# A four-layer graph network: straight-line programs, and one fp32 incidence product per graph

## The chip, the cores and the metric

The kernel runs on one core of one Trainium2 chip. The metric is device microseconds of one execution. The median of three runs before the change is 1470.65 us (1470.1 to 1474.69).

## What is computed

128 graphs of 128 nodes, 256 features each (x), and an adjacency matrix per graph (adj, 128x128). Four graph layers follow one another, each added to its input and normalised over the features:

```python
x = _layernorm(x + L0(x, adj))   # hypergraph convolution, relu, layer norm, second convolution
x = _layernorm(x + L1(x, adj))   # mean over neighbours, concatenated with x, weighted, relu
x = _layernorm(x + L2(x, adj))   # three graph convolutions
x = _layernorm(x + L3(x, adj))   # one graph convolution, relu, mask
```

The change touches the incidence part of L0. With H = (adj != 0) and w the first row of adj, the reference forms

```python
Dn = jnp.einsum('nce,ne->nc', H, w)      # node degrees
Dn = jnp.where(Dn > 0, 1.0 / Dn, 0.0)
Be = H.sum(axis=1)                       # edge sizes
Be = jnp.where(Be > 0, 1.0 / Be, 0.0)
```

and applies Dn * H * Be * H^T twice. The kernel computes the 128x128 matrix G = H * (Be * H^T) once per graph, together with the degrees as one more column, scales its rows by Dn and uses the result (GT, transposed) in both convolutions.

## The kernel before, in words

Graphs are worked in 64 pairs. The kernel is a software pipeline: in step n each stage works on pair n - LAG[stage] (lines 22 to 26), from G at lag 0 to the last norm F at lag 5. Step 0 to 2 fill the pipeline by hand (`fill` of each engine), and `body(n, k)` is one full step, with the operations of each engine written in a fixed order; nothing reorders them. Engines meet through semaphores that count pairs.

`steps` (line 185) lays the steps out: fill, then steps 3 to 7 written out, then a hardware loop over steps 8 to 59 whose body holds four steps, then steps 60 to 68 written out. Inside the loop a pair's number is a register's value; `begun`, `upto`, `first`, `active`, `bank` and `at_count` tell the two cases apart by `isinstance(pair, int)`, and SP's loads and stores address memory with it.

TensorE's order in a step is R, G, xT, H2W, Ax2, XAB, H1, AP3, P, Tr, AXB, H1W, Ax3, Gx, GP, H2, TK. All matmuls but the transposes are issued in `mm` (line 279). Two kinds occur. Rounded products (fp32r) come as hi and lo parts, three terms each (`product`). Full fp32 products take unsplit operands: Ax2, Ax3, H2, Gx, GP. G (line 307) is of the rounded kind with two terms, H (exact in fp32r) against BH hi and BH lo, 130 columns: 128 of Be * H^T, the weight w, and a column of zeros.

The operands of G(n+1) are made in step n. VectorE: `edges` writes HT (line 903), `edge_count` sums it (907), `w_high_edge_max` copies w rounded into BH (911) and takes the maximum with 1 (913), `edge_inverse` takes the inverse (921), the rest of w (923) and splits the inverse in three operations (925, 927, 928). They are interleaved with `degree_max`, `degree_recip`, `degree_inverse` and `make_Gd` of step n. GpSimd: `make_BH` (line 1233) multiplies HT by the two parts of the inverse in two operations.

What follows in a step and is named later: VectorE adds up the third norm's input behind AP3 (line 1133, n_s), computes statistics and n_shift (847); ScalarE applies the norm, giving x3 (`apply`, 586), which TensorE's Ax3 reads; then h_mean (649) on ScalarE, h_var (945) and h_veps (948) on VectorE, h_std (653) on ScalarE, h_rstd and p_f (964) on VectorE, and TensorE's GP reads p_f. GpSimd works in its order: r_lo twice, two sums of squares, A_lo, n_s (1282), h_lo, BH, x2c (1293), xb (1243), h_lo. ScalarE's `copy_A` stands before `out_XAB`, whose first copy is xbw_hi.

Of the kernel before, what the change touches and what calls it, by code (L numbers as in the profile page):

```python
# [7 lines left out]
ALU = mybir.AluOpType  # L8
# [20 lines left out]
UNROLL = 4  # L29
FIRST_IN_LOOP = 8  # L30


def build(nc, x, adjT, w1T, w2T, wab, v1, v2, v3, wk, columns, rows, eye, out):
# [3 lines left out]
    assert (C, GP_, D, DH) == (128, 2, 256, 512) and NP % UNROLL == 0 and NP > FIRST_IN_LOOP  # L37
    END = NP + LAG["F"]

    with ExitStack() as ctx:  # L40
# [30 lines left out]
        HT = sb("HT", [2, C], F32R)  # L71
        ht_count, be = sb("ht_count", [2]), sb("be", [2])
        be_r, be_parts = sb("be_r", [2], F32R), sb("be_parts", [2, 2])

        BH = sb("BH", [2, 2, C + 2], F32R)
# [34 lines left out]
        class Norm:  # L110
# [25 lines left out]
        ht_made, ht_counted, be_max, be_made, be_hi, be_lo, bh_made = (  # L136
            sem(s) for s in ("ht_made", "ht_counted", "be_max", "be_made", "be_hi", "be_lo", "bh_made"))
        dn_1, dn_2, dn_3, gd_made = sem("dn_1"), sem("dn_2"), sem("dn_3"), sem("gd_made")
        w_hi, w_lo, gt_made, gx_hi, gx_lo = (sem(s) for s in ("w_hi", "w_lo", "gt_made", "gx_hi", "gx_lo"))
# [18 lines left out]
        def begun(pair):  # L158

            return not isinstance(pair, int) or pair >= 0  # L160

        def upto(pair):

            return min(pair, NP - 1) + 1 if isinstance(pair, int) else pair + 1

        def first(n, j):

            return isinstance(n, int) and n == j

        def active(stage, n):  # L170
            return not isinstance(n, int) or 0 <= n - LAG[stage] < NP

        def bank(stage, pair):

            filling = isinstance(pair, int)
            if filling and stage == "Tr" and pair in (1, 2):
                return 3
            if filling and stage == "GP" and pair == 0:
                return 2
            if filling and stage == "xT" and pair == 0:  # L180
                return 6
            return BANK[stage]

        def steps(eng, fill, body):

            stop = NP - UNROLL
            fill()
            for n in range(FILL, FIRST_IN_LOOP):
                body(n, n)
            with eng.Fori(FIRST_IN_LOOP, stop - UNROLL + 1, UNROLL) as base:  # L190
                for k in range(UNROLL):
                    body(base + k, k)
            for n in range(stop, END):
                body(n, n)

        def at_count(p, k):

            if isinstance(p, int):
                return 16 * (p // RING + 1)
            return (p + (RING - k % RING)) * (16 // RING)  # L200
# [12 lines left out]
        def _(sp):  # L213
# [4 lines left out]
            def input_free(p):  # L218
                sp.wait_ge(pe_did["Gx"], upto(p))
                sp.wait_ge(xb_made, upto(p))  # L220
                sp.wait_ge(pe_did["G"], upto(p))
                sp.wait_ge(w_lo, upto(p))
                sp.wait_ge(a_copied, upto(p))
                sp.wait_ge(a_lo, upto(p))
# [22 lines left out]
            def body(n, k):  # L247
                if not isinstance(n, int) or n + 2 < NP:
                    input_free(n - 2)
                    if isinstance(n, int):  # L250
                        load(n + 2)
                    else:
                        sp.dma_start(at_in[:, (k + 2) % RING],
                                     adjT[bass.ds(n + 2, 1)].rearrange("a p g c -> p (a g) c")
                                     ).then_inc(at_loaded[(k + 2) % RING], 16)
                        sp.dma_start(x_in[:, (k + 2) % RING],
                                     x[bass.ds(n + 2, 1)].rearrange("a p g c -> p (a g) c")
                                     ).then_inc(x_loaded[(k + 2) % RING], 16)
                if active("F", n):
                    p = n - LAG["F"]  # L260
                    sp.wait_ge(n4.done, upto(p))
                    src = x4[(k - LAG["F"]) % 2]
                    if isinstance(p, int):
                        sp.dma_start(out[p], src[:]).then_inc(stored[(k - 5) % 2], 16)
                    else:
                        sp.dma_start(out[bass.ds(p, 1)].rearrange("a p g c -> p (a g) c"),
                                     src[:]).then_inc(stored[(k - 5) % 2], 16)

            steps(sp, fill, body)
# [5 lines left out]
        def _(pe):  # L275
# [285 lines left out]
            steps(pe, fill, body)  # L561
# [3 lines left out]
        def _(act):  # L565
# [99 lines left out]

            def split_w1(h):
                half = slice(h * 2 * C, (h + 1) * 2 * C)
                act.wait_ge(w1_loaded[h], 16)
                copy(w1T_s[0][:, :, half], w1T_f[:, :, half]).then_inc(w1_hi, 1)

            def fill():
                act.wait_ge(consts_step, 1)
                act.activation(h_std[:, 0:1], eps_c[:], ACT.Sqrt).then_inc(table_loaded, 1)
                act.wait_ge(table_loaded, 1)
                act.wait_ge(columns_loaded, 16)
# [3 lines left out]
                split_w1(1)  # L679

# [6 lines left out]
                split_gx(1, 1)  # L687
                copy_A(1, 1)
# [17 lines left out]
                split_gx(2, 2)  # L706
                act.wait_ge(v_loaded, 16 * 4)
# [8 lines left out]
            def body(n, k):  # L716
# [64 lines left out]
                if active("F", n):  # L781
                    p = n - 5
                    if not isinstance(p, int):
                        act.wait_ge(stored[(k - 5) % 2], (p - (k - 5) % 2) * 8)
                    elif p >= 2:
                        act.wait_ge(stored[p % 2], 16 * (p // 2))
                    apply(n4, p, x4[(k - 5) % 2])
# [23 lines left out]
            steps(act, fill, body)  # L811
# [3 lines left out]
        def _(dve):  # L815
# [60 lines left out]
            g_dn = psum[:, BANK["G"], 0:2 * (C + 2)].rearrange("p (g c) -> p g c", g=2)  # L876
# [28 lines left out]
            def edge_count(n, k):  # L905
                dve.wait_ge(ht_made, upto(n + 1))
                dve.tensor_reduce(ht_count[:], f(HT[:]), AX_X, ALU.add).then_inc(ht_counted, 1)

            def w_high_edge_max(n, k):
                q = n + 1  # L910
                dve.tensor_copy(BH[:, 0, :, C:C + 1], at_in[:, (k + 1) % RING, :, 0:1]).then_inc(w_hi, 1)
                dve.wait_ge(ht_counted, upto(q))
                dve.tensor_scalar(be[:], ht_count[:], 1.0, None, ALU.max).then_inc(be_max, 1)

            def edge_inverse(n, k):
                q = n + 1
                w = at_in[:, (k + 1) % RING, :, 0:1]
# [12 lines left out]
            def prep(n, k):  # L930
                edges(n, k)
                edge_count(n, k)
                w_high_edge_max(n, k)
# [77 lines left out]
            def fill():  # L1011
# [6 lines left out]
                for h in range(2):  # L1018
                    dve.tensor_scalar(xbw[1][:, :, D + h:D + h + 1], pair01, 0.0, None, ALU.mult)
                    dve.tensor_scalar(BH[:, h, :, C + 1:C + 2], pair01, 0.0, None, ALU.mult)  # L1020
# [66 lines left out]
            def body(n, k):  # L1087
# [32 lines left out]
                if active("prep", n):  # L1120
                    w_high_edge_max(n, k)
# [77 lines left out]
            steps(dve, fill, body)  # L1199
# [3 lines left out]
        def _(pool):  # L1203
# [97 lines left out]
            steps(pool, fill, body)  # L1301
# [42 lines left out]
```

## Time and profile before

| | us |
|---|---|
| median of three runs | 1470.65 |
| the profiled execution | 1472.7 |
| its span | 1470.8 |
| TensorE matmul busy | 1420.3 (97%) |
| VectorE busy | 1151.5 (78%) |
| ScalarE busy | 1051.4 (71%) |
| GpSimd busy | 889.0 (60%) |
| DMA, mean | 31 GB/s |

Busy times are shares of the whole span, with the filling (some 70 us) and the emptying (some 90 us) in them. Matmuls overlap in the record, so two starts tell more than a duration. Times in rows are us from the span's start; the number behind the time is the operation's own length.

### The profile page before, as it was taken

To read this page: it belongs to the slowest core of one execution; us is meant where nothing else is said; L and a number is where in the kernel's file an instruction comes from. 1 tells how busy PE (TensorE), PEld (TensorE's weight loads), DVE (VectorE), ACT (ScalarE), POOL (GpSimd) and SP (SyncE) were. 2 spreads that over 40 slices of the span, in tenths; PEclk is the share of its full clock that TensorE was granted. 3 is DMA by queue.
4 is the path that set the end of the run, shared out by engine and by line. 5 is a ranking of instruction groups with operands and counts; after the bars stand their busy time and mean duration, and the time that the engine had idled before them with its cause. 6 is when DMAs were issued, how large, how long until landed. Compare 5 with 4: busy or idle time off the path is not lost. (4 is left out here: it accounts for less than half of the span.)

```text
span 1470.8 us, 34536 instructions
## 1 busy us (share of the span) xinstructions
PE 1420.3 (97%) x10896; PEld 1355.6 (92%) x10896; DVE 1151.5 (78%) x4066; ACT 1051.4 (71%) x2378; POOL 889.0 (60%) x840
## 2 busy tenths in 40 slices
PE   6899999999999999999999999999999999999974
PEld 6799999999999999999999999999999999999973
DVE  6678878878878888788788788788787887887663
ACT  3577777777777777777777777777777767777853
POOL 4565675675575576566566566566566566567532
PEclk9999999999999999999999999999999999999997
DMA  4001101101101101101101101100100110110000
GB/s 135 23 12 37 37 20 37 36 18 36 36 18 36 36 18 36 36 18 36 36 18 36 36 19 34 36 25 29 36 28 25 36 30 23 36 36 9 16 15 22
DMA packets 29819, 45.45 MB, mean 31 GB/s; under 512 B 3408, under 2 KB 12240, under 8 KB 29776
## 3 DMA queue, kind: packets, MB, share of 16 engines
q1 hardware_dynamic: 29776, 44.91, 9.7%
q8 instruction: 22, 0.36, 0.1%
q14 instruction: 21, 0.17, 0.0%
HBM read 28.12 MB, written 16.78 MB: 31 GB/s over the span
## 5 line engine op out<-in xcount | busy, mean ns | idle before, releaser
L1205 POOL TENSOR_TENSOR h_lo<-h_f,h_hi 128x512 fp32r<-128x512 f32 x128 | 165.2, 1291 | 339.9 <-ACT h_hi L567 339.9
L586 ACT ACTIVATE x<-n_s,n_shift,n_rstd 128x256 f32<-128x256 f32 x384 | 208.6, 591 | 65.9 <-DVE n_shift L847 63.1
L825 DVE BATCH_NORM_STATS2 n_st<-n_s 128x6 f32<-128x256 f32 x512 | 188.1, 409 | 7.6 <-POOL n_s L1282 5.2
L581 ACT ACTIVATE n_std<-n_mv,eps_c 128x2 f32<-128x2 f32 x256 | 74.8, 292 | 158.9 <-DVE n_mv L830 158.8
L1213 POOL TENSOR_TENSOR r_lo<-r_f,r_hi 128x512 fp32r<-128x512 f32 x128 | 164.0, 1304 | 38.2 <-ACT r_hi L567 38.1
L1274 POOL TENSOR_TENSOR n_s<-tk,mask 128x512 f32<-128x512 f32 x64 | 66.7, 1042 | 168.4 <-issue 82.6
L279 PE MATMUL psum<-v_hi,h_hi 128*128 128x256 f32 x512 | 149.4, 292 | 4.9 <-issue 4.9
L591 ACT ACTIVATE h_f<-psum,columns 128x256 f32<-128x256 f32 x256 | 107.6, 472 | 54.2 <-PE psum L279 54.2
L279 PE MATMUL psum<-w2c_hi,r_hi 128*128 128x258 f32 x512 | 145.0, 283 | 0.9 <-POOL r_lo L1213 0.9
L279 PE MATMUL psum<-v_lo,h_hi 128*128 128x256 f32 x512 | 145.3, 284 | 0.0
L279 PE MATMUL psum<-w2c_hi,r_lo 128*128 128x258 f32 x512 | 144.8, 283 | 0.0
L279 PE MATMUL psum<-v_hi,h_lo 128*128 128x256 f32 x512 | 144.8, 283 | 0.0
L279 PE MATMUL psum<-w2c_lo,r_hi 128*128 128x258 f32 x512 | 144.8, 283 | 0.0
L279 PE MATMUL psum<-gx_hi,w1T_hi 128*128 128x256 f32 x512 | 143.9, 281 | 0.0
L279 PE MATMUL psum<-A_f,x 128*128 128x128 f32 x1024 | 137.7, 278 | 5.9 <-ACT x L586 4.8
L279 PE MATMUL psum<-gx_lo,w1T_hi 128*128 128x256 f32 x512 | 143.3, 280 | 0.0
L279 PE MATMUL psum<-gx_hi,w1T_lo 128*128 128x256 f32 x512 | 143.3, 280 | 0.0
L279 PEld LDWEIGHTS psum<-A_f,x 128*128 128x128 f32 x1024 | 127.3, 194 | 6.5 <-ACT x L586 5.2
L817 DVE TENSOR_TENSOR ax_lo<-psum,ax_hi 128x512 fp32r<-128x512 f32 x128 | 87.8, 686 | 27.1 <-ACT ax_hi L567 27.1
L279 PE MATMUL psum<-wab_hi,x1T_hi 128*128 128x512 f32 x256 | 107.4, 419 | 0.0
L279 PEld LDWEIGHTS psum<-v_hi,h_hi 128*128 128x128 f32 x512 | 97.8, 191 | 5.5 <-issue 5.5
L591 ACT ACTIVATE r_f<-psum,columns 128x256 f32<-128x256 f32 x256 | 99.1, 463 | 4.1 <-PE psum L279 4.1
(146 smaller groups left out, 5113.5 us busy)
## 6 DMA issues: line engine op xcount, KB each, us to landing
x_in<-x_in_dram SPq DMA_DIRECT2D x64, 256.0 KB, 2.7
out<-x SPq DMA_DIRECT2D x64, 256.0 KB, 2.0
at_in<-adjT SPq DMA_DIRECT2D x64, 128.0 KB, 2.1
x<-v_in SPq DMA_DIRECT2D x3, 256.0 KB, 5.9
n_s<-w2T_in SPq DMA_DIRECT2D x2, 256.0 KB, 3.2
r_f<-w1T_in SPq DMA_DIRECT2D x2, 256.0 KB, 4.7
h_f<-wab_in SPq DMA_DIRECT2D x2, 256.0 KB, 5.9
rows<-rows_in SPq DMA_DIRECT2D x1, 256.0 KB, 5.9
```

What stands on the lines that cost most here:

```text
L279: return pe.matmul(o, a, b, start=start, stop=stop)
L581: act.activation(nm.std[:], nm.mv[:, :, 1], ACT.Sqrt, bias=eps_c[:, 0:1]).then_inc(nm.rooted, 1)
L586: last = act.activation(dst[:, g, :], nm.s[:, g, :], ACT.Identity, scale=nm.rstd[:, g:g + 1], bias=nm.shift[:, g:g + 1])
L591: return act.activation(dst[:, m].rearrange("p g c -> p (g c)"), psum[:, BANK[stage] + extra, (m % 2) * 2 * C:(m % 2 + 1) * 2 * C], ACT.Re ...
L817: return dve.tensor_tensor(dst[1][:], src, f(dst[0][:]), ALU.subtract).then_inc(signal, 1)
L825: last = dve.bn_stats(nm.st[:, g, :], nm.s[:, g, :])
L1205: return pool.tensor_tensor(dst[1][:], src, f(dst[0][:]), ALU.subtract).then_inc(signal, 1)
L1213: pool.tensor_tensor(r_s[1][:, half], r_f[:, half], f(r_s[0][:, half]), ALU.subtract).then_inc(r_lo[h], 1)
L1274: pool.tensor_tensor(n4.s[:], tk[:], bc(mask[:], [C, 2, D], 2), ALU.mult).then_inc(tk_masked, 1)
```

## The change

`steps` writes every step out on every engine, so every pair's number is a constant. G becomes one full fp32 product per graph on an unrounded HT and an unrounded BH of 129 columns. VectorE no longer splits w and the inverse; GpSimd makes BH in one operation; the copy of w into BH moves to ScalarE (`weight_column`, behind `copy_A` in a step, and at four places of its fill). The diff, shortened:

```diff
-        HT = sb("HT", [2, C], F32R)
-        ht_count, be = sb("ht_count", [2]), sb("be", [2])
-        be_r, be_parts = sb("be_r", [2], F32R), sb("be_parts", [2, 2])
-        BH = sb("BH", [2, 2, C + 2], F32R)
+        HT = sb("HT", [2, C])
+        ht_count, be, be_inv = sb("ht_count", [2]), sb("be", [2]), sb("be_inv", [2])
+        BH = sb("BH", [2, C + 1])
...
-        def steps(eng, fill, body):
-            stop = NP - UNROLL
+        def steps(fill, body):
             fill()
-            for n in range(FILL, FIRST_IN_LOOP):
+            for n in range(FILL, END):
                 body(n, n)
-            with eng.Fori(FIRST_IN_LOOP, stop - UNROLL + 1, UNROLL) as base:
-                for k in range(UNROLL):
-                    body(base + k, k)
-            for n in range(stop, END):
-                body(n, n)
...
         # SP, input_free
-                sp.wait_ge(w_lo, upto(p))
+                sp.wait_ge(w_made, upto(p))
...
         # TensorE, G
-                pe.wait_ge(w_lo, upto(p))
+                pe.wait_ge(w_made, upto(p))
...
-                    o = psum[:, BANK["G"], g * (C + 2):(g + 1) * (C + 2)]
-                    mm(o, HT[:, g, :], BH[:, 0, g, :], True, False)
-                    last = mm(o, HT[:, g, :], BH[:, 1, g, :], False, True)
+                    last = mm(psum[:, BANK["G"], g * (C + 1):(g + 1) * (C + 1)], HT[:, g, :], BH[:, g, :],
+                              True, True)
...
+            def weight_column(n, k):
+                q = n + 1
+                act.wait_ge(at_loaded[(k + 1) % RING], at_count(q, k + 1))
+                if begun(n):
+                    act.wait_ge(pe_did["G"], upto(n))
+                copy(BH[:, :, C:C + 1], at_in[:, (k + 1) % RING, :, 0:1]).then_inc(w_made, 1)
...
         # ScalarE, body
                 if active("R", n):
                     square_r(n, k)
                     copy_A(n, k)
+                if active("prep", n):
+                    weight_column(n, k)
                 if active("XAB", n):
                     out_XAB(n, k)
...
-            def w_high_edge_max(n, k):
+            def edge_max(n, k):
                 q = n + 1
-                dve.tensor_copy(BH[:, 0, :, C:C + 1], at_in[:, (k + 1) % RING, :, 0:1]).then_inc(w_hi, 1)
                 dve.wait_ge(ht_counted, upto(q))
                 dve.tensor_scalar(be[:], ht_count[:], 1.0, None, ALU.max).then_inc(be_max, 1)
             def edge_inverse(n, k):
...
-                dve.reciprocal(be_parts[:, 1, :], be[:]).then_inc(be_made, 1)
-                dve.wait_ge(w_hi, upto(q))
-                dve.tensor_tensor(BH[:, 1, :, C:C + 1], w, f(BH[:, 0, :, C:C + 1]), ALU.subtract).then_inc(w_lo, 1)
-                dve.wait_ge(be_made, upto(q))
-                dve.tensor_copy(be_r[:], be_parts[:, 1, :]).then_inc(be_hi, 1)
-                dve.wait_ge(be_hi, upto(q))
-                dve.tensor_copy(be_parts[:, 0, :], f(be_r[:]))
-                dve.tensor_tensor(be_parts[:, 1, :], be_parts[:, 1, :], f(be_r[:]), ALU.subtract).then_inc(be_lo, 1)
+                dve.reciprocal(be_inv[:], be[:]).then_inc(be_made, 1)
...
         # GpSimd, make_BH
-                pool.wait_ge(be_lo, upto(q))
+                pool.wait_ge(be_made, upto(q))
...
-                for h in range(2):
-                    last = pool.tensor_tensor(BH[:, h, :, 0:C], f(HT[:]), bc(be_parts[:, h, :], [C, 2, C], 2),
-                                              ALU.mult)
-                last.then_inc(bh_made, 1)
+                pool.tensor_tensor(BH[:, :, 0:C], HT[:], bc(be_inv[:], [C, 2, C], 2), ALU.mult).then_inc(bh_made, 1)
```

The fill of ScalarE calls `weight_column` for pairs 0, 1, 2 and 3: ahead of its wait for the columns, behind `split_w1(1)`, behind `split_gx(1, 1)` and behind `split_gx(2, 2)`. Two VectorE operations of the fill that cleared the zero column of BH go.

## Rows read from the trace of the kernel before

**Rows 1.** Busy time by stretch: us, each engine's busy us, clock, DMA.
```profile
661.00:749.50 88.50, 88.36 (x688) 84.49 (x687) 72.12 (x255) 65.94 (x151) 55.05 (x52) 1.00 0.09 30
```

**Rows 2.** Timeline, VectorE, line 1133: start us, length us, operation.
```profile
126.94 0.69 DVE L1133 TENSOR_TENSOR n_s<-psum,x2c 128x512 f32<-128x512 f32 x1
148.76 0.69 DVE L1133 TENSOR_TENSOR n_s<-psum,x2c 128x512 f32<-128x512 f32 x1
...
1332.43 0.69 DVE L1133 TENSOR_TENSOR n_s<-psum,x2c 128x512 f32<-128x512 f32 x1
...
1376.07 0.69 DVE L1133 TENSOR_TENSOR n_s<-psum,x2c 128x512 f32<-128x512 f32 x1 [2.49 <-PE psum L279]
```

**Rows 3.** Timeline, TensorE, Gx and H2 of an ordinary step and of step 63.
```profile
725.20 1.06 PE L279 MATMUL psum<-GT,x_in 128*128 128x128 f32 x8
...
727.20 1.05 PE L279 MATMUL psum<-A_f,h1w 128*128 128x128 f32 x8
...
1382.41 1.06 PE L279 MATMUL psum<-GT,x_in 128*128 128x128 f32 x8
...
1384.17 1.05 PE L279 MATMUL psum<-A_f,h1w 128*128 128x128 f32 x8
```

**Rows 4.** Timeline, VectorE, the same ordinary step.
```profile
722.06 0.29 DVE L847 SCALAR_TENSOR_TENSOR n_shift<-n_mv,n_rstd 128x2 f32<-128x2 f32 x1
...
724.03 0.80 DVE L948 SCALAR_TENSOR_TENSOR h_veps<-h_var,eps_c 128x2 f32<-128x2 f32 x1
...
725.31 0.88 DVE L964 SCALAR_TENSOR_TENSOR p_f<-psum,h_rstd,betaW 128x256 f32<-128x256 f32 x2
```

**Rows 5.** Timeline, GpSimd, the same step.
```profile
721.14 1.20 POOL L1233 TENSOR_TENSOR BH<-HT,be_parts 128x256 fp32r<-128x256 f32 x2
...
723.54 1.27 POOL L1243 TENSOR_TENSOR xb<-x_in,b2half 128x512 f32<-128x512 f32 x1
```

**Rows 6.** DMA queues: packets, MB, share of 16 engines.
```profile
q8 instruction: 22, 0.36, 0.1%
```

**Rows 7.** Timeline, TensorE, G and xT, then Ax2 up to XAB.
```profile
710.51 0.56 PE L279 MATMUL psum<-BH,HT 128*128 128x130 f32 x4
710.91 0.65 PE L394 MATMUL psum<-ident,x 128*128 128x128 f32 x4
...
712.83 1.05 PE L279 MATMUL psum<-A_f,x 128*128 128x128 f32 x8
713.64 0.47 PE L279 MATMUL psum<-wab_hi,x1T_hi 128*128 128x512 f32 x1
```

**Rows 8.** Timeline, VectorE, from the copy of w to line 1133.
```profile
716.47 0.74 DVE L911 CAST BH<-at_in 128x2 fp32r<-128x2 f32 x1
...
718.63 0.15 DVE L928 TENSOR_TENSOR be_parts<-be_parts,be_r 128x2 f32<-128x2 f32 x1
718.86 0.69 DVE L1133 TENSOR_TENSOR n_s<-psum,x2c 128x512 f32<-128x512 f32 x1
```

**Rows 9.** Timeline, ScalarE, copy_A's second copy and the operation behind it.
```profile
715.85 0.44 ACT L567 ACTIVATE A_f<-at_in 128x256 f32<-128x256 f32 x1
716.72 0.60 ACT L567 ACTIVATE xbw_hi<-psum 128x512 fp32r<-128x512 f32 x1 [0.43 <-PE psum L279]
```

**Rows 10.** Timeline, GpSimd and VectorE, step 63, which makes no BH.
```profile
1378.30 1.30 POOL L1293 TENSOR_TENSOR x2c<-x,rows 128x512 f32<-128x512 f32 x1
...
1379.27 0.35 DVE L847 SCALAR_TENSOR_TENSOR n_shift<-n_mv,n_rstd 128x2 f32<-128x2 f32 x1
...
1381.30 0.16 DVE L948 SCALAR_TENSOR_TENSOR h_veps<-h_var,eps_c 128x2 f32<-128x2 f32 x1
```

**Rows 11.** Timeline, GpSimd and TensorE, the first 20 us.
```profile
4.62 1.19 POOL L1233 TENSOR_TENSOR BH<-HT,be_parts 128x256 fp32r<-128x256 f32 x2 [4.16 <-DVE be_parts L928]
...
16.95 2.55 POOL L1233 TENSOR_TENSOR BH<-HT,be_parts 128x256 fp32r<-128x256 f32 x2 [11.14 <-DVE be_parts L928]
...
19.55 0.66 PE L279 MATMUL psum<-BH,HT 128*128 128x130 f32 x4 [1.70 <-POOL BH L1233]
```

More of the change, by code:

```diff
@@ L28 @@
 FILL = 3
-UNROLL = 4
-FIRST_IN_LOOP = 8
 def build(nc, x, adjT, w1T, w2T, wab, v1, v2, v3, wk, columns, rows, eye, out):
@@ L36, in build @@
     KD, KH = D // C, DH // C
-    assert (C, GP_, D, DH) == (128, 2, 256, 512) and NP % UNROLL == 0 and NP > FIRST_IN_LOOP
+    assert (C, GP_, D, DH) == (128, 2, 256, 512) and NP % 2 == 0 and NP > 8
     END = NP + LAG["F"]
@@ L135, in build @@
         pe_R0 = sem("pe_R0")
-        ht_made, ht_counted, be_max, be_made, be_hi, be_lo, bh_made = (
-            sem(s) for s in ("ht_made", "ht_counted", "be_max", "be_made", "be_hi", "be_lo", "bh_made"))
+        ht_made, ht_counted, be_max, be_made, bh_made = (
+            sem(s) for s in ("ht_made", "ht_counted", "be_max", "be_made", "bh_made"))
         dn_1, dn_2, dn_3, gd_made = sem("dn_1"), sem("dn_2"), sem("dn_3"), sem("gd_made")
-        w_hi, w_lo, gt_made, gx_hi, gx_lo = (sem(s) for s in ("w_hi", "w_lo", "gt_made", "gx_hi", "gx_lo"))
+        w_made, gt_made, gx_hi, gx_lo = (sem(s) for s in ("w_made", "gt_made", "gx_hi", "gx_lo"))
         r_relu, r_hi = [sem(f"r_relu{j}") for j in range(2)], [sem(f"r_hi{j}") for j in range(2)]
@@ L158, in begun @@
         def begun(pair):
-            return not isinstance(pair, int) or pair >= 0
+            return pair >= 0
         def upto(pair):
-            return min(pair, NP - 1) + 1 if isinstance(pair, int) else pair + 1
+            return min(pair, NP - 1) + 1
         def first(n, j):
-            return isinstance(n, int) and n == j
+            return n == j
         def active(stage, n):
-            return not isinstance(n, int) or 0 <= n - LAG[stage] < NP
+            return 0 <= n - LAG[stage] < NP
         def bank(stage, pair):
-            filling = isinstance(pair, int)
-            if filling and stage == "Tr" and pair in (1, 2):
+            if stage == "Tr" and pair in (1, 2):
                 return 3
-            if filling and stage == "GP" and pair == 0:
+            if stage == "GP" and pair == 0:
                 return 2
-            if filling and stage == "xT" and pair == 0:
+            if stage == "xT" and pair == 0:
                 return 6
             return BANK[stage]
-        def steps(eng, fill, body):
-            stop = NP - UNROLL
+        def steps(fill, body):
             fill()
-            for n in range(FILL, FIRST_IN_LOOP):
-                body(n, n)
-            with eng.Fori(FIRST_IN_LOOP, stop - UNROLL + 1, UNROLL) as base:
-                for k in range(UNROLL):
-                    body(base + k, k)
-            for n in range(stop, END):
+            for n in range(FILL, END):
                 body(n, n)
         def at_count(p, k):
-            if isinstance(p, int):
-                return 16 * (p // RING + 1)
-            return (p + (RING - k % RING)) * (16 // RING)
+            return 16 * (p // RING + 1)
         def f(ap):
@@ L247, in body @@
             def body(n, k):
-                if not isinstance(n, int) or n + 2 < NP:
+                if n + 2 < NP:
                     input_free(n - 2)
[L250 to L258, printed above, removed]
+                    load(n + 2)
                 if active("F", n):
@@ L261, in body @@
                     sp.wait_ge(n4.done, upto(p))
[L262 to L269, printed above, removed]
+                    sp.dma_start(out[p], x4[p % 2][:]).then_inc(stored[p % 2], 16)
+            steps(fill, body)
             for j in range(2):
@@ L559, in body @@
                     TK(n, k)
-            steps(pe, fill, body)
+            steps(fill, body)
         @block.scalar
@@ L674, in fill @@
                 act.wait_ge(table_loaded, 1)
+                weight_column(-1, -1)
                 act.wait_ge(columns_loaded, 16)
@@ L679, in fill @@
                 split_w1(1)
+                weight_column(0, 0)
                 relu_r(1, 1, 0)
@@ L687, in fill @@
                 split_gx(1, 1)
+                weight_column(1, 1)
                 copy_A(1, 1)
@@ L706, in fill @@
                 split_gx(2, 2)
+                weight_column(2, 2)
                 act.wait_ge(v_loaded, 16 * 4)
@@ L782, in body @@
                     p = n - 5
-                    if not isinstance(p, int):
-                        act.wait_ge(stored[(k - 5) % 2], (p - (k - 5) % 2) * 8)
-                    elif p >= 2:
+                    if p >= 2:
                         act.wait_ge(stored[p % 2], 16 * (p // 2))
@@ L809, in body @@
                     root(n1, n - 1)
-            steps(act, fill, body)
+            steps(fill, body)
         @block.vector
@@ L874, in split_xbw @@
                                   f(xbw[0][:, :, 0:D]), ALU.subtract).then_inc(xbw_lo, 1)
-            g_dn = psum[:, BANK["G"], 0:2 * (C + 2)].rearrange("p (g c) -> p g c", g=2)
+            g_dn = psum[:, BANK["G"], 0:2 * (C + 1)].rearrange("p (g c) -> p g c", g=2)
             dn = g_dn[:, :, C]
@@ L906, in edge_count @@
                 dve.wait_ge(ht_made, upto(n + 1))
-                dve.tensor_reduce(ht_count[:], f(HT[:]), AX_X, ALU.add).then_inc(ht_counted, 1)
-            def w_high_edge_max(n, k):
+                dve.tensor_reduce(ht_count[:], HT[:], AX_X, ALU.add).then_inc(ht_counted, 1)
+            def edge_max(n, k):
                 q = n + 1
-                dve.tensor_copy(BH[:, 0, :, C:C + 1], at_in[:, (k + 1) % RING, :, 0:1]).then_inc(w_hi, 1)
                 dve.wait_ge(ht_counted, upto(q))
@@ L916, in edge_inverse @@
                 q = n + 1
-                w = at_in[:, (k + 1) % RING, :, 0:1]
                 dve.wait_ge(be_max, upto(q))
@@ L932, in prep @@
                 edge_count(n, k)
-                w_high_edge_max(n, k)
+                edge_max(n, k)
                 edge_inverse(n, k)
@@ L1019, in fill @@
                     dve.tensor_scalar(xbw[1][:, :, D + h:D + h + 1], pair01, 0.0, None, ALU.mult)
-                    dve.tensor_scalar(BH[:, h, :, C + 1:C + 2], pair01, 0.0, None, ALU.mult)
                 dve.tensor_copy(w2c_s[0][:, :, D:D + 1], four01)
@@ L1120, in body @@
                 if active("prep", n):
-                    w_high_edge_max(n, k)
+                    edge_max(n, k)
                 if active("G", n):
@@ L1197, in body @@
                     shift(n2, n - 2)
-            steps(dve, fill, body)
+            steps(fill, body)
         @block.gpsimd
@@ L1299, in body @@
                     lo(h2_s, h2_f[:], h2_lo)
-            steps(pool, fill, body)
+            steps(fill, body)
 def kernel(x, adj, L0_gnn_W1, L0_gnn_b1, L0_gnn_gamma, L0_gnn_beta, L0_gnn_W2, L0_gnn_b2, L1_gnn_W,
```

## The prediction

> **What bounds the kernel now.** I read the busy time by stretch first. In four steps in the middle of the run TensorE's matmuls are busy for 88.36 of 88.50 us at full clock [rows 1]: the steady part is one unbroken matmul stream, and work taken from VectorE, ScalarE or GpSimd is worth only what it takes out of that stream.
>
> Then the length of a step. The operation at line 1133 (the third norm's sum) runs once per step, always just behind the last matmul of the stage AP3, so it is a clock tick of TensorE [rows 2]. Counting steps as the code's n, the four ticks shown are steps 6, 7, 61 and 63. Steps up to 7 and from 60 on are written out. From 6 to 7 the trace has 148.76 - 126.94 = 21.82 us, from 61 to 63 it has 43.64, again **21.82 us per step**. From 7 to 61 are 54 steps, 52 of them the loop's, in 1332.43 - 148.76 = 1183.67 us, 21.92 each. Inside the loop a step is 0.10 us longer on average.
>
> Last, whether those 21.82 us hold idle time. They do, at one place. From the first matmul of Gx to the first of H2 (across GP) an ordinary step takes 727.20 - 725.20 = 2.00 us; the last step that runs these products takes 1384.17 - 1382.41 = 1.76 us [rows 3]. The missing 0.24 us is GP waiting for p_f, which VectorE makes at 725.31 and ends 0.88 us later [rows 4]. Why p_f is late shows in three rows that fit to 0.01 us. n_shift, two numbers a lane from SBUF, starts at 722.06 and ends at 722.35; GpSimd's second BH operation ends at 721.14 + 1.20 = 722.34 [rows 4, 5]. h_veps starts at 724.03 and ends at 724.83; GpSimd's xb ends at 723.54 + 1.27 = 724.81. Such small VectorE operations stand still until the GpSimd operation under way is over. n_shift gates ScalarE's x3, behind which h_mean, h_var, h_veps, h_std, h_rstd and p_f follow in a row.
>
> **The change, part by part.**
>
> *Loop written out.* 54 steps at 21.82 would be 1178.28 us; they take 1183.67 [rows 2]. Written-out steps, with the same instructions, run at 21.82 on either side of it. So **-5.4 us**. Against it stands that the instructions no longer repeat, and all 64 steps are fetched. The larger instruction queue now moves 22 packets, 0.36 MB [rows 6], for three filling steps, five written out, four in the loop and nine at the end; later it is about four times that, 1 GB/s, and the written-out steps, which have that traffic already, show no price for it. Bounds: nothing, up to the whole 5.4 given back.
>
> *G on TensorE.* Before: 2 graphs x 2 terms, 4 matmul records of 130 columns, 710.51 to 710.91, 0.40 us. After: 2 fp32 products of 129 columns. An fp32 product appears as two records: Ax2 has 4 products and shows x8, in 713.64 - 712.83 = 0.81 us [rows 7], 0.101 us a record. Four records again: 4 x 0.101 = 0.40 us, plus one column in 128. **0 us.** The Trainium skill (FP8 and Floating Point Precision, TensorE Precision Notes) counts true fp32 as four passes through the array. At one column a cycle that would be 4 x 129 columns a graph against 2 x 130 before, and 0.22 us more a step; the row gives the narrow rounded products no such advantage, so I keep to the row.
>
> *VectorE.* It loses per step the copy of w (0.74 us), the rest of w, and three operations that split the inverse, the last of which ends at 718.78 [rows 8]. All lie before the tick at 718.86, and the tick does not move: it waits for AP3, also in the last step where VectorE had stood idle for 2.49 us before it [rows 2]. **0 us**, hidden by TensorE. Everything on VectorE behind the tick keeps its place, n_shift at tick + 3.20 in particular.
>
> *ScalarE.* One more copy of 128x2 behind copy_A, whose own copy of 128x256 takes 0.44 us; the narrow one is bounded by that. ScalarE then stands idle for 0.43 us before xbw_hi, waiting for XAB on TensorE [rows 9]. **0 us**; if that cover were gone, up to 0.44 us on xbw_hi, for which AXB waits. Its waits (at_in of the next pair, G of this one) are long over: nothing queues behind it. SP's inputs wait for w_made in place of w_lo, a semaphore of two steps ago: 0.
>
> *GpSimd, and this is the delicate one.* One BH operation in place of two: -0.6 us in front of x2c and xb. Counting from the tick at 718.86: BH +2.28 to +2.89, x2c then about +2.84 to +4.13 (1.30 long in [rows 10], starting 0.05 before BH's end is recorded), xb +4.08 to +5.35. n_shift comes at +3.20. Before, a short BH was running and let it go at +3.49. Now x2c is running, and it goes at about **+4.14**: 0.65 us later. From the end of n_shift to the start of h_veps lay 724.03 - 722.35 = 1.68 us, so h_veps starts at +5.82. Now xb is over (+5.35), and h_veps takes its bare 0.16 us (as in the last step, at 1381.30 [rows 10]) where it took 0.80: it ends at +5.98. Before, it ended at 724.83, +5.97. **Two shifts of 0.65 cancel, 0.0 us per step**, p_f and GP stay. That this mechanism works with x2c is seen in the last step, which has no BH: x2c ends at 1378.30 + 1.30 = 1379.60 and n_shift, waiting since 1379.27, at 1379.62 [rows 10]. The Trainium skill (SBUF — State Buffer, on the engine side's shared port pair) has the rule for it: VectorE with two SBUF inputs and GpSimd lock the pair for the whole instruction, and the loser blocks fully. By that rule no gap opens inside x2c, and the trace agrees; a split of bandwidth would only have stretched n_shift a little. x3 is 0.65 later too, done near +5.4, about when Ax3 begins (I put that wait at 0.1 us at most; it lies ahead of GP and comes off the wait that GP has anyway). Bounds for this term: the whole stall gone, -0.24 x 60 = -14 us; or 0.1 us more a step, +6.
>
> *Filling the pipeline.* The first G waits for BH, two operations in 1.19 us at 4.62 [rows 11]: one goes (-0.6), and three VectorE splits before it, which I put at 0.15 us each by the one at 718.63 [rows 8] (-0.45), so -1.05 us. The chain behind is serial up to the second BH. That starts at 16.95, takes 2.55 (slowed by a large VectorE operation) and TensorE idles 1.70 us for it, starting G at 19.55 [rows 11]. After: -1.05, -0.5 for the splits, -1.27 for one of two: G at about 16.75, -2.8; ScalarE's GT copy behind its squares gives 0.3 back. **-2.5 us**, if the loads are in by then. Bounds -1 and -4.
>
> *Sum:* -5.4 + 0 + 0 + 0 + 0.0 - 2.5 = -7.9 us. The profiled execution took 1472.7 us (span 1470.8); the median of the runs is 1470.65, 2.05 below it. So 1464.8 against the profiled one and **1463 us** as a median.
>
> **Rivals.**
>
> *A: the stall at GP goes.* If n_shift gets in between BH and x2c, or BH ends late enough (0.3 us) to cover it, h_veps is free at xb's end, p_f comes 0.5 us earlier, and each step loses 0.24 us: 60 x 0.24 = 14.4, giving 1449. For it: the last step ran so. Against it: there x2c happened to end at +3.53; here it is to end at +4.13. 0.18.
>
> *B: the chain over x3 gets longer.* n_shift's delay is fully paid, and the gain at h_veps is smaller, or Ax3 waits visibly: 0.1 us x 60 = +6, giving 1469, no change that can be told. For it: the cancellation is of two numbers of 0.65, and any new GpSimd boundary can catch another small operation. 0.12.
>
> *C: the fp32 product is dearer than the rows of Ax2 say (slower).* The place is G, on the stream that has no slack. If an fp32 product of an odd 129 columns takes four record times and not two, 4 more of 0.101 us come in each step: 64 x 0.40 = +26, less 7.9, giving 1489. It decides from 7.9/64 = 0.12 us per step on. Against it: Ax2 at 128 columns streams at two records a product [rows 7]. The Trainium skill's four passes, named above, would give +14 and 1477. 0.07.
>
> *D: straight code doesn't save the 5.4 us.* If fetching pages costs what the branches cost, only the filling gains: 1468. The written-out steps speak against it [rows 2]. 0.05.
>
> **How the numbers follow.** Forecast 0.58, A 0.18, B 0.12, C 0.07, D 0.05. A measurement tells 0.3% (4.4 us) from no change. The forecast is 0.5% faster and its own bounds (fill -1 to -4, chain within 0.04 us a step) reach from 1459 to 1467, so 0.56 of its 0.58 counts as faster, with all of A: 0.74. Same: B, D and the rest, 0.17. Slower: C and a worse B, 0.09. The range takes in A and B, 1446 to 1469.
>
> **What will show it.** Right: ticks of line 1133 all 21.82 us apart; BH in 4 records within 0.40 us; n_shift ending with x2c, about 0.9 us long; h_veps 0.16 us; GP still behind p_f by the same wait; G of the second pair near 17 us. Wrong: steps of 21.58 (A), of 21.9 (B), of 22.0 or more with more records under BH (C), or of 21.92 (D).

## The result

Over seven runs each the median went from 1470.65 us to **1463.80 us** (1462.21 to 1466.07); the ratio is 0.9949, 95% interval 0.9938 to 0.9960, that is 5.9 to 9.1 us faster. Forecast were 1463 and a range of 1446 to 1469. The profiled execution took 1463.48 us, 9.2 below the one before, which had lain 2 us above its median.

The busy table of the kernel after (share of the span, instructions) and its DMA queues:

```profile
span 1461.7 us, 33281 instructions
...
PE 1416.2 (97%) x10896; PEld 1353.8 (93%) x10896; DVE 1080.4 (74%) x3744; ACT 1056.8 (72%) x2442; POOL 851.7 (58%) x776
...
q8 instruction: 89, 1.46, 0.4%
q14 instruction: 81, 0.66, 0.2%
```

TensorE issues the same 10896 matmul records. VectorE lost 322 instructions and 71 us of busy time, GpSimd 64 and 37 us, and hardly any of this shows in the total. Instructions are fetched by two queues of their own, q8 and q14; q8 moves four times the packets of [rows 6], 89 for 22, and q14 81 where it moved 21.

The ticks of the third norm's sum, as in [rows 2] (steps 6, 7, 11, 12, 13, 61, 63):

```profile
124.53 0.69 DVE L1108 TENSOR_TENSOR n_s<-psum,x2c 128x512 f32<-128x512 f32 x1 [1.25 <-PE psum L254]
146.36 0.69 DVE L1108 TENSOR_TENSOR n_s<-psum,x2c 128x512 f32<-128x512 f32 x1 [1.25 <-PE psum L254]
...
233.69 0.69 DVE L1108 TENSOR_TENSOR n_s<-psum,x2c 128x512 f32<-128x512 f32 x1 [1.25 <-PE psum L254]
255.62 0.69 DVE L1108 TENSOR_TENSOR n_s<-psum,x2c 128x512 f32<-128x512 f32 x1 [1.26 <-PE psum L254]
277.46 0.69 DVE L1108 TENSOR_TENSOR n_s<-psum,x2c 128x512 f32<-128x512 f32 x1 [1.25 <-PE psum L254]
...
1325.98 0.69 DVE L1108 TENSOR_TENSOR n_s<-psum,x2c 128x512 f32<-128x512 f32 x1 [1.25 <-PE psum L254]
...
1369.66 0.69 DVE L1108 TENSOR_TENSOR n_s<-psum,x2c 128x512 f32<-128x512 f32 x1 [2.47 <-PE psum L254]
```

VectorE now stands idle 1.25 us ahead of each tick: that is where its relief went. Tick 7 is at 146.36 where it was at 148.76, so the fill gave **2.4 us**. From tick 7 to 61 it is 1179.62 us where it was 1183.67: **4.05 us**, 21.84 us a step. Behind tick 63 there were 1470.8 - 1376.07 = 94.7 us, now 1461.7 - 1369.66 = 92.0: **2.7 us** that no step of the prediction had. The three sum to the span's 9.1. That the fill and the end also hold chance is told under e8 and e12.

One ordinary step of the kernel after, VectorE, GpSimd, ScalarE and TensorE in turn (the tick is at 736.03):

```profile
739.23 0.97 DVE L832 SCALAR_TENSOR_TENSOR n_shift<-n_mv,n_rstd 128x2 f32<-128x2 f32 x1
741.88 0.16 DVE L924 SCALAR_TENSOR_TENSOR h_veps<-h_var,eps_c 128x2 f32<-128x2 f32 x1
742.51 0.88 DVE L940 SCALAR_TENSOR_TENSOR p_f<-psum,h_rstd,betaW 128x256 f32<-128x256 f32 x2
...
738.31 0.63 POOL L1207 TENSOR_TENSOR BH<-HT,be_inv 128x256 f32<-128x256 f32 x1
738.88 1.30 POOL L1265 TENSOR_TENSOR x2c<-x,rows 128x512 f32<-128x512 f32 x1
740.12 1.30 POOL L1215 TENSOR_TENSOR xb<-x_in,b2half 128x512 f32<-128x512 f32 x1
...
733.34 0.23 ACT L541 ACTIVATE BH<-at_in 128x2 f32<-128x2 f32 x1
733.90 0.60 ACT L541 ACTIVATE xbw_hi<-psum 128x512 fp32r<-128x512 f32 x1 [0.33 <-PE psum L254]
...
727.70 0.61 PE L254 MATMUL psum<-BH,HT 128*128 128x129 f32 x4
728.14 0.60 PE L368 MATMUL psum<-ident,x 128*128 128x128 f32 x4
```

n_shift waits out x2c (738.88 + 1.30 = 740.18; n_shift ends at 740.20, tick + 4.17), h_veps finds GpSimd done and takes 0.16 us, and ends at tick + 6.01. Before, these were + 3.49, 0.80 us and + 5.97. The exchange is as forecast. The new copy takes 0.23 us and ScalarE still idles 0.33 behind it. G is four records, starting 0.44 us ahead of xT where it was 0.40. x3 is late by as much as n_shift, and Ax3 does wait for it: in the median of the ordinary steps Gx, the next product, starts at tick + 6.43 where it was + 6.34. GP still waits for p_f, so these 0.09 us come off its wait.

### The profile page after: what moved, and what is told of

Read it like the earlier page. It is cut to its first block and busy times, and to the rows that moved or that the text cites. A ratio compares the mean times of both kernels' runs of the same rounds, so it can differ in the third digit from the quotient of the medians.

```text
span 1461.7 us, 33281 instructions
## 1 busy us (share of the span) xinstructions
PE 1416.2 (97%) x10896; PEld 1353.8 (93%) x10896; DVE 1080.4 (74%) x3744; ACT 1056.8 (72%) x2442; POOL 851.7 (58%) x776
## 5 line engine op out<-in xcount | busy, mean ns | idle before, releaser
L254 PE MATMUL psum<-A_f,x 128*128 128x128 f32 x1024 | 142.1, 282 | 5.4 <-ACT x L560 4.8
L1108 DVE TENSOR_TENSOR n_s<-psum,x2c 128x512 f32<-128x512 f32 x64 | 44.3, 692 | 87.0 <-PE psum L254 87.0
```

The source lines that it names most:

```text
L254: return pe.matmul(o, a, b, start=start, stop=stop)
L1108: dve.tensor_tensor(n3.s[:].rearrange("p g d -> p (g d)"), flat(BANK["AP3"]), x2c[(k - 4) % 2][:].rearrange("p g d -> p (g d)"), ALU.add). ...
```

## The experiments

Each is compared with runs of the kernel before on the same chip, whose median there was between 1469.7 and 1472.9; step times come from the ticks.

**e1, the loop alone.** The kernel before with this edit and the old G:

```diff
-            for n in range(FILL, FIRST_IN_LOOP):
+            for n in range(FILL, END):
                 body(n, n)
-            with eng.Fori(FIRST_IN_LOOP, stop - UNROLL + 1, UNROLL) as base: ...
-            for n in range(stop, END): ...
```

> The kernel before with every step written out and nothing else changed. My theory (the loop costs 5.4 us spread over its steps, by three waits in the first step behind each branch): the ticks of line 1133 lie 21.82 us apart throughout, steps 7 to 61 take 1178.3 us in place of 1183.7, the median is 5.4 us below before, 1465.3. Rival (page fetching eats it, or the 22.1 us steps have another cause than the branch): 1470 to 1471, with long steps left.

Measured: 1468.18 us, ratio 0.9980 (0.9969 to 0.9990). Its ticks 7 and 61:

```profile
149.19 0.69 DVE L1127 TENSOR_TENSOR n_s<-psum,x2c 128x512 f32<-128x512 f32 x1
...
1327.71 0.69 DVE L1127 TENSOR_TENSOR n_s<-psum,x2c 128x512 f32<-128x512 f32 x1
```

1178.52 us for the 54 steps, as forecast (1178.3), and the long steps at every fourth place are gone. The whole run gained less, 1.5 to 4.6 us by the interval; the profile has 5.2 in the steps and 1.1 behind tick 63, less 0.4 in the fill. Part of the rest is TensorE's clock: the mean granted clock of the eleven runs is 0.9891, of the fifteen of before 0.9901, which is up to 1.5 us of a run (an estimate), and the trace's clock record has two stretches of 6.8 us at half clock in the fill of this run's profile, where before has two of 3.4. The remainder stays open.

**e2, G alone, with the loop.** The kernel after with the loop of before over steps 8 to 59, and the loop's register forms of the loads, stores and waits:

```diff
-            for n in range(FILL, END):
-                body(n, n)
+            for n in range(FILL, FIRST_IN_LOOP):
+                body(n, n)
+            with eng.Fori(FIRST_IN_LOOP, stop - UNROLL + 1, UNROLL) as base: ...
+            for n in range(stop, END): ...
```

> The kernel after with the hardware loop over steps 8 to 59 put back. My theory (the parts add, and the G part is worth its 2.4 us in the fill, with ordinary steps 0.02 us longer): the 7th tick is at about 146.4 as after, steps 7 to 61 take some 1185 us, the median is 1.5 to 2.5 us below before, 1468 to 1469. Rival (the G part alone also shortens or lengthens each step): 1455 or 1475.

Measured: **1507.55 us**, ratio 1.0253 (1.0233 to 1.0273). Both theories missed it by far. Two steps in four are the 21.83 of after, but the first behind each branch back takes 24.5 to 26.2, twelve in all. VectorE and TensorE around one such place:

```profile
427.35 0.13 DVE L858 SCALAR_TENSOR_TENSOR n_shift<-n_mv,n_rstd 128x2 f32<-128x2 f32 x1
430.63 0.17 DVE L854 RECIPROCAL n_rstd<-n_std 128x2 f32<-128x2 f32 x1 [3.15 <-issue]
...
432.87 0.42 DVE L1097 TENSOR_SCALAR_CACHE_REDUCE nz<-x 128x256 f32<-128x256 f32 x1 [1.23 <-issue]
...
431.70 0.66 PE L392 MATMUL psum<-ident,x 128*128 128x128 f32 x4 [2.62 <-DVE x L868]
```

And its second queue of instruction packets (packets, MB, share):

```profile
q14 instruction: 80, 0.66, 0.1%
```

The first operation of VectorE's body comes 3.15 us late, released by nothing that the profile shows, and xT on TensorE waits 2.62 us for x1. Part of the loss is the clock. Behind this idle time TensorE is granted half its clock for 3.4 us (busy table by stretch; the clock is the third number from the end):

```profile
429.00:432.50 3.50, 0.88 (x8) 0.80 (x8) 0.90 (x3) 1.65 (x6) 0.00 (x0) 1.00 0.01 2
432.50:435.90 3.40, 3.40 (x18) 3.40 (x18) 1.99 (x7) 2.09 (x4) 1.84 (x2) 0.50 0.01 2
```

Eight of the twelve long steps hold such a stretch and take 26.0 to 26.2 us; the four without take 24.5 to 24.7.

The second instruction queue moves 80 packets where the kernel before moved 21 for the same number of written-out steps: the loop fetches instructions anew on every round. Yet VectorE's body is *shorter* than before, 303 recorded instructions for 323. So a new theory: instructions are fetched in packets of fixed size (pages; here 0.66 MB in 80 packets, 8 KB each), and not the body's length but its place against their boundaries decides whether every round fetches it anew.

**e5 and e6, only the place moved.** e5 is e2 with 47, e6 the kernel before with 77 one-column memsets of VectorE in the fill, ahead of the loop. The edit of e5 against e2 (e6 has 40 and 37 at the same two places):

```diff
+                for j in range(24):
+                    dve.memset(pads[:, j:j + 1], 0.0)
                 dve.wait_ge(w2_sums, 1)
...
+                for j in range(24, 47):
+                    dve.memset(pads[:, j:j + 1], 0.0)
                 dve.wait_ge(betaW_sums, 1)
```

> The kernel of the run with the loop put back (1507.6), plus 47 tiny VectorE memsets in the fill, ahead of the loop. They move the loop's place in VectorE's program back to about where the kernel before had it; its body stays 303 recorded instructions. My theory (each branch of VectorE waits some 3 us for instruction pages because of where the body lies against page boundaries, not because of its length or of what it computes): the instruction packets of the second queue fall from 80 to about 21, the steps of 24.5 to 26.2 us become 22.1 to 22.3, and the time is 1468 to 1472 (the memsets add up to 3 us). Rival (something in the new G makes the first step behind a branch long): still about 1507.

> The kernel before plus 77 tiny VectorE memsets in the fill, which move its loop by 0.6 of a page of 128 instructions. My theory (place against the pages): its VectorE body of 323 now also straddles one page too many, the second queue's packets rise from 21 to about 80, each branch costs some 3 to 4 us more, 13 x 3 = 39, 1505 to 1515. Rival (only the changed G brings the long steps): 1471 to 1475, the price of the memsets alone.

Measured: e5 **1470.64 us** (ratio 0.9983, 0.9973 to 0.9994), e6 **1511.86 us** (ratio 1.0273, 1.0250 to 1.0296). The second instruction queue of e5:

```profile
q14 instruction: 21, 0.17, 0.0%
```

The same of e6:

```profile
q14 instruction: 82, 0.67, 0.2%
```

Instructions that do nothing, placed ahead of the loop, take 37 us away in one kernel and add 39 to the other; from tick 7 to 61 it is 1184.50 us for e2's 1223.89, and 1223.33 for before's 1183.67. So it is the place of the body, neither its length nor the new G: the loop of the kernel before was cheap by where it lay. That boundaries of pages are what the place is measured against is not shown, since only one amount of padding was tried in each kernel.

e5 is also what e2 was meant to be, G with a loop that stays cheap: its median is 2.3 us below before's on the same chip, as e2's first theory had it.

**e3, the fp32 product's price.** The kernel after with G's products issued twice:

```diff
-                for g in range(2):
+                for g in (0, 1, 0, 1):
                     last = mm(psum[:, BANK["G"], ...], HT[:, g, :], BH[:, g, :], True, True)
```

> The kernel after with both fp32 products of G issued a second time (the same result). If an fp32 product of 129 columns costs two records of 0.101 us, and TensorE's stream has no slack before AP3: +0.40 us per step, 64 x 0.40 = 26 us, 1490. If each costs four record times: +0.80 us per step, 1515. If G lies beside other work: no change.

Measured: 1481.73 us, ratio 1.0074 (1.0057 to 1.0091), which is 18 us above after for the 26 expected. G and the start of xT:

```profile
734.24 1.05 PE L254 MATMUL psum<-BH,HT 128*128 128x129 f32 x8
735.13 0.60 PE L368 MATMUL psum<-ident,x 128*128 128x128 f32 x4
```

G takes 0.89 us for 0.44. Ticks lie 22.11 us apart, only 0.27 more. GP's weights load at tick + 7.24 and not + 7.41, since BH, x2c and xb start some 0.16 us earlier against a tick that moved back (tick + 2.13 for + 2.29): 0.27 + 0.17 = 0.44 us for two products more, four record times of 0.11. Two records a product, 0.22 us, and not four; the wait at GP swallowed the rest.

That leaves why the old product of 130 columns was no cheaper, 0.40 us for four records [rows 7]. The kernel before also has fp32 products of a single column, here four records and the start of what follows:

```profile
721.54 0.50 PE L279 MATMUL psum<-ones,sq 128*128 128x1 f32 x4
721.91 0.42 PE L329 MATMUL psum<-ident,Gd 128*128 128x128 f32 x2
```

They take 0.37 us, and a rounded record of 256 columns takes 0.12. So a record costs some 0.1 us in this kernel however narrow it is; what sets that isn't shown.

**e4, the wait at GP taken away.** The kernel after with one GpSimd operation moved:

```diff
-                if active("prep", n):
-                    make_BH(n, k)
                 if active("x2", n): ...
                 if active("GP", n):
                     make_xb(n, k)
+                if active("prep", n):
+                    make_BH(n, k)
```

> The kernel after with GpSimd's BH moved behind x2c and xb in every step. My theory (GP waits for p_f because n_shift, and in the kernel before also h_veps, stand still behind a GpSimd operation): x2c ends at tick + 3.5, n_shift with it, h_veps finds GpSimd idle or in BH for at most 0.3 us, p_f at about + 5.9, GP's wait is gone, a step takes 21.58 to 21.62 us, and the median is 0.24 x 57 = 14 us below after, 1450. Rival (the wait at GP has another cause, or the next G now waits for BH): 1464 or more.

Measured: **1447.67 us**, ratio to before 0.9843 (0.9826 to 0.9860), 16 us below after. One step from its tick on, VectorE, GpSimd and TensorE:

```profile
728.25 0.69 DVE L1108 TENSOR_TENSOR n_s<-psum,x2c 128x512 f32<-128x512 f32 x1 [1.47 <-PE psum L254]
731.45 0.22 DVE L832 SCALAR_TENSOR_TENSOR n_shift<-n_mv,n_rstd 128x2 f32<-128x2 f32 x1
733.35 0.16 DVE L924 SCALAR_TENSOR_TENSOR h_veps<-h_var,eps_c 128x2 f32<-128x2 f32 x1
733.99 0.88 DVE L940 SCALAR_TENSOR_TENSOR p_f<-psum,h_rstd,betaW 128x256 f32<-128x256 f32 x2
...
730.39 1.27 POOL L1263 TENSOR_TENSOR x2c<-x,rows 128x512 f32<-128x512 f32 x1
731.62 1.29 POOL L1215 TENSOR_TENSOR xb<-x_in,b2half 128x512 f32<-128x512 f32 x1
732.87 0.61 POOL L1207 TENSOR_TENSOR BH<-HT,be_inv 128x256 f32<-128x256 f32 x1
...
734.60 1.06 PE L254 MATMUL psum<-GT,x_in 128*128 128x128 f32 x8
735.49 1.03 PE L254 MATMUL psum<-p_f,GT 128*128 128x256 f32 x4
736.36 1.05 PE L254 MATMUL psum<-A_f,h1w 128*128 128x128 f32 x8
```

p_f starts at tick + 5.74 for + 6.48, Gx to H2 takes 1.76 us, the figure of step 63 in [rows 3], and every step takes 21.56 us. This is the fastest of all kernels here.

**e10, the same in the kernel before**, with its two operations and its loop:

> The kernel before, loop and rounded G kept, with GpSimd's two BH operations moved behind x2c and xb. My theory: n_shift ends with x2c at tick + 3.5, h_veps at + 5.1 waits at most for the first BH operation (+ 5.25), GP's wait is gone in ordinary steps, 21.56 to 21.6 us each, only the steps behind a branch stay longer (about 21.9): 14 us below before, 1456 to 1459 where before shows 1470 to 1473. Rival (the wait comes back because h_veps waits for both operations, + 5.85, as late as after): 1470.

Measured: 1453.70 us, ratio 0.9873 (0.9851 to 0.9894). Its ticks 7, 11, 12 and 61:

```profile
148.59 0.69 DVE L1133 TENSOR_TENSOR n_s<-psum,x2c 128x512 f32<-128x512 f32 x1 [0.30 <-PE psum L279]
...
234.85 0.69 DVE L1133 TENSOR_TENSOR n_s<-psum,x2c 128x512 f32<-128x512 f32 x1 [0.30 <-PE psum L279]
256.41 0.69 DVE L1133 TENSOR_TENSOR n_s<-psum,x2c 128x512 f32<-128x512 f32 x1
...
1313.18 0.69 DVE L1133 TENSOR_TENSOR n_s<-psum,x2c 128x512 f32<-128x512 f32 x1 [0.30 <-PE psum L279]
```

54 steps in 1164.59 us; e4, without a loop, has 1164.24. The step with the branch is 256.41 - 234.85 = 21.56 us long, like the others: the 5.4 us that the loop cost go when GP's wait goes. They were there only because a delay of a few tenths at each branch met a chain without slack. I had expected 21.9 there. The 6 us by which the whole run is above e4's do not lie in the steps: 2.5 are in the fill (tick 7 at 148.59 for 146.13) and 2.8 behind tick 63, which is clock (e8 and e12).

**e7, GpSimd's half microsecond put back.** The kernel after with a second product of BH's shape, into a spare tile, ahead of BH:

```diff
+                pool.tensor_tensor(BH_spare[:], HT[:], bc(be_inv[:], [C, 2, C], 2), ALU.mult)
                 pool.tensor_tensor(BH[:, :, 0:C], HT[:], bc(be_inv[:], [C, 2, C], 2), ALU.mult).then_inc(bh_made, 1)
```

> The kernel after with a second GpSimd product of BH's shape, into a spare tile, ahead of BH. My theory (with one BH the wait of n_shift grows by as much as h_veps's shrinks): x2c and xb are 0.57 us later, n_shift ends at tick + 3.49 and takes 0.29 us again, h_veps waits for xb (0.80), p_f at + 6.44, steps of 21.81 to 21.82 in place of 21.84, and the time is 1 us below to 1 us above after's 1463.8. Rival (GpSimd's half microsecond matters by itself): 1475 or more if it were on the path at its length, 57 x 0.57 = 32 us.

Measured: 1465.34 us, ratio 0.9949 (0.9933 to 0.9964), and 1178.41 us from tick 7 to 61, 1.2 below after. Making BH twice on GpSimd is not slower in the steps. n_shift takes 0.30 us and h_veps 0.80 again (tick at 736.43):

```profile
739.63 0.30 DVE L833 SCALAR_TENSOR_TENSOR n_shift<-n_mv,n_rstd 128x2 f32<-128x2 f32 x1
...
741.62 0.80 DVE L925 SCALAR_TENSOR_TENSOR h_veps<-h_var,eps_c 128x2 f32<-128x2 f32 x1
```

The 21.82 us of this step, with the fp32 G in it, also say that the 0.44 us for 0.40 at G isn't paid.

**e9 and e11, VectorE's five operations put back.** The kernel after with three copies and two subtractions into spare tiles; e9 has all five ahead of the inverse, e11 at the places where the kernel before had its own (one ahead of the maximum, four behind the inverse):

```diff
+                dve.tensor_copy(spare[2][:], w)
+                dve.tensor_tensor(spare[3][:], w, w, ALU.subtract)
+                dve.tensor_tensor(spare[4][:], w, w, ALU.subtract)
...
                 dve.reciprocal(be_inv[:], be[:]).then_inc(be_made, 1)
```

> The kernel after with five small VectorE operations put back ahead of the inverse (three copies and two subtractions of w's shape into spare tiles). My theory (VectorE's relief is worth nothing in a step, since line 1133 waits for AP3, and some of the fill's gain is these operations): steps of 21.84 as after, tick 7 about 0.5 to 1 us later than after's 146.4, 1464 to 1465. Rival (the relief counts): 5 x 0.15 to 0.7 us a step on the path, at least 57 x 0.8 = 45 us, 1509.

> The kernel after with five small VectorE operations put back at the places where the kernel before had its own: a copy ahead of the maximum, the rest behind the inverse, so that GpSimd's BH is not held. My theory (the relief is worth nothing as long as the last of them ends before AP3 does, and here it must, as it did in the kernel before, some 0.1 us ahead): steps of 21.84, tick 7 at 146.4, 1463 to 1466. Rival (they cost whenever they are there, as in the run with five ahead of the inverse): steps of 23.07, 1535. Between: the last one misses the end of a GpSimd operation and waits for n_s (1.29 us), steps of about 23.

Measured: e9 **1535.76 us** (ratio 1.0427, 1.0407 to 1.0447), steps of 23.07; e11 1462.84 us (ratio 0.9940, 0.9920 to 0.9961), 1179.33 us from tick 7 to 61, as after. e9, VectorE and GpSimd up to the tick:

```profile
564.13 0.15 DVE L909 TENSOR_TENSOR spare<-at_in 128x2 f32<-128x2 f32 x1
564.20 1.25 DVE L910 TENSOR_TENSOR spare<-at_in 128x2 f32<-128x2 f32 x1
565.38 0.15 DVE L911 RECIPROCAL be_inv<-be 128x2 f32<-128x2 f32 x1
565.45 0.66 DVE L1115 TENSOR_TENSOR n_s<-psum,x2c 128x512 f32<-128x512 f32 x1
...
564.14 1.29 POOL L1261 TENSOR_TENSOR n_s<-n_s,x 128x512 f32<-128x512 f32 x1
```

The last of the five has two columns. It slips behind the start of GpSimd's n_s and waits out all of it (564.14 + 1.29 = 565.43; it ends at 565.45), and the tick, till then a clock of TensorE, is now VectorE's. Each step costs 1.23 us more for one missed boundary. In their old places the same five are free, though the last of them ends only 0.08 us ahead of the tick.

**e8 and e12, before and after once more**, for the stretch behind tick 63:

> The kernel before once more, for a second profile. The steps should repeat to 0.02 us (steps 7 to 61 in 1183.7 us). If the 2 us by which its profiled execution lies above the median are TensorE's clock while the pipeline empties, this profile shows either the same half-clock stretches and 94.8 us behind tick 63, or none between and 92 us.

> The kernel after once more, for a second profile. Steps of 21.84 (steps 7 to 61 in 1179.6 us), tick 7 at 146.4 give or take 3 us of half-clock stretches, and behind tick 63 either 92.0 us as before or, if the clock there is chance, up to 95.

Measured: e8 1472.15 us (ratio 0.9988, 0.9977 to 0.9999), e12 1463.89 us (ratio 0.9944, 0.9924 to 0.9964). e8 is the kernel before against itself, and its interval leaves out 1: a difference of 0.1 or 0.2% in a whole run, as in e1 and e5, is not told by the interval, only by the ticks. The runs of before lie mostly in two groups, near 1470 us at granted clocks of 0.990 to 0.994 and near 1474 to 1475 at 0.987 to 0.988, and how many a set has of each moves its median. The steps repeat: 1183.71 and 1179.26 us from tick 7 to 61. Behind tick 63 before has 94.9 us again (first 94.7), after 93.4 (first 92.0). The trace's clock record has two stretches of 3.4 us at half clock in the first 50 us behind tick 63 in both profiles of before, none in the first of after and one in the second. The whole stretch behind tick 63, first profile of each, before and then after:

```profile
1376.07:1470.80 94.73, 65.65 (x460) 61.44 (x458) 49.69 (x184) 50.13 (x109) 35.35 (x30) 0.88 0.05 17
1369.66:1461.70 92.04, 63.00 (x460) 58.54 (x458) 49.64 (x184) 50.10 (x109) 35.29 (x30) 0.92 0.05 18
```

The same 460 matmul records at a granted clock of 0.88 and of 0.92. Over all fourteen profiles the time behind tick 63 goes by the number of these stretches: 92.0 to 92.4 us with none (after, e2, e4, e9, e11), 93.3 to 93.8 with one (e1, e3, e5, e6, e12), 94.8 to 95.4 with two (before, e7, e8, e10). e7, the kernel after with one more GpSimd operation, has two and e2, with the loop, none, so neither the new G nor the straight program decides it alone.

In the fill, tick 7 of before came at 151.8 in e8 for 148.8, again with one half-clock stretch more and one twice as long. The fill of after has one stretch of 6.8 us where before has 3.4; e2, with after's fill and two stretches of 3.4, reaches tick 7 at 145.60, 3.2 us ahead of before. So the first pair of profiles flattered the change by 1 to 3 us at the end and may have hidden up to 1 in the fill. Why both profiles of before have two stretches at the end, and those of after fewer, isn't shown.

## Why the prediction was right

The sum was -7.9 us; the ratio gives -5.9 to -9.1, the medians -6.85.

- *Loop, -5.4.* By itself confirmed in the steps (e1: -5.2; e1's whole runs show 1.5 to 4.6), though the reason given in the sum was incomplete: it isn't a price of the loop but one of the chain that it meets (e10). Of "against it", the fetching of four times the instructions, nothing shows in ordinary steps.
- *G, 0.* Confirmed. Rival C's four record times per product are excluded by e3 (0.44 us for two products). The Trainium skill's four passes, taken at a column a cycle, had meant 0.22 us a step. The four passes themselves agree with the traces: 4 x 129 columns at 2.4 GHz would be 0.215 us, and e3 has 0.22 a product; in e4, where GP doesn't wait, its two products of 256 columns take 736.36 - 735.49 = 0.87 us, and 8 x 256 columns would be 0.85 (estimates). What fails is the column a cycle for the old product, whose narrow records took 0.10 us each (e3). G was free because the old one was dear for its width, not because fp32 is cheap.
- *VectorE, 0.* Confirmed by 1.25 us of idle before each tick and by e11. But in the kernel before "hidden by TensorE" held by 0.1 us only; e9 shows what stood behind it.
- *ScalarE, 0.* Confirmed: 0.23 us within an idle 0.56.
- *GpSimd, 0.0.* The term that mattered most. n_shift's end was forecast at + 4.14 and came at + 4.17, h_veps ended at + 6.01 for + 5.98, and p_f's lateness is 0.04 us more than before. This makes the step 21.84 in place of 21.82, 54 x 0.02 = 1.1 us: with it, -5.4 becomes the -4.05 measured, but for 0.3 in a few single longer steps. e7 turns it back. Rival B's mechanism is there, then, but at 0.02 us a step and not 0.1; Ax3's wait, put at 0.1 us at most, is 0.09, and comes off the wait at GP as said.
- *Fill, -2.5.* Measured -2.4, with the clock's share in it (-3.2 by e2). The second G began at 16.90 us, forecast 16.75.
- The 2.7 us behind tick 63 were not in the sum; they are clock, and mostly offset by the 2 us by which before's profiled run lay above its median. Each term of the sum came within 1.1 us; that the median came within 1 us of the forecast is in part luck, since the half-clock stretches alone move a run by more.
- Rival A's -14 us did not come by this change, but is the right size: e4 got 16 us below after by it.
- What the list of rivals lacked: that with the loop kept the same G costs 37 us (e2). Measured alone the halves are about -3 and +37, and -7 together. With the padding of e5 they are -3 and -2.5 and nearly add up, so what doesn't add is the place of the loop.

## What to carry to other kernels

Where VectorE and GpSimd both run, a two-column VectorE operation can take as long as the GpSimd operation under way; find the small ones on the critical chain and order GpSimd so that none of its long ones begins just ahead of them. Moving one GpSimd operation by two places gave over twice what the whole change gave. And before judging an edit inside a hardware loop, count the instruction packets: if they grow with the rounds (here 80 for 21), the body is fetched anew each time, and the time says little about the edit itself; some padding ahead of the loop tells the two apart.

## What was unexpected of the hardware

A branch can cost a step a few tenths of a microsecond, or hold VectorE for 3.15 and TensorE for 2.62, depending on 47 or 77 idle instructions that lie ahead of the loop (21 packets or 80 to 82). The idle time can then cost TensorE its clock as well: 0.50 for 3.4 us in eight of twelve rounds of e2. The Trainium skill (Runtime: NRT & Kernel Launch, Instruction fetch mechanics) has it that a taken branch whose target has left the instruction window forces a fetch by DMA before the engine goes on; e2 and e6 agree, with 3 us or so for each (39 us over twelve branches back, the clock's part included). That the body's place, and not its length, decides is from e5 and e6.
